# One core, Mamba front end: where the x projection, the high parts, GpSimd's blocks and the statistics stand in the chunk's order

## The reference

```python
x = x + mamba(group_norm(x), ...)        # layer 0
x = x + memory(group_norm(x), m)         # layer 1
```

```python
xn = layer_norm(xf) * ln_w + ln_b                 # 512 channels
xin, z = split(xn @ in_proj_w.T)                  # 1024 channels each
xs = silu(causal_conv4(xin) + conv_b)             # called u in the kernel
x_dbl = xs @ x_proj_w.T                           # 32 columns dt, 16 B, 16 C
delta = softplus(dt @ dt_proj_w.T + dt_proj_b)
# handed on: delta, delta * u, u, silu(z), B, C   -> selective scan, gating, out projection
```

## Time and profile before

| | |
|---|---|
| median of 3 runs | 4889.37 us (4878.66 to 4891.94) |
| the profiled execution's own time | 4877.88 us |
| its span in the trace | 4876.2 us |
| busy: TensorE, VectorE, GpSimd, ScalarE | 95%, 85%, 69%, 61% |
| `front`, from its first projection to the last x_dbl | 73.6 to 1101 us of the span |
| mean granted TensorE clock | 0.984 |

### The profile page before, as it was taken

The page is one execution under the profiler, slowest core; times in us unless marked ns, Lnnn a source line. Parts: engine busy times, 40 slices in busy tenths (PEclk is TensorE's granted clock), DMA queues, the critical chain, the costliest instruction groups (busy, mean ns, idle before and its releaser), DMA issues. The chain is left out here.

```text
span 4876.2 us, 120012 instructions
## 1 busy us (share of the span) xinstructions
PE 4630.9 (95%) x47164; PEld 2943.1 (60%) x47164; DVE 4121.5 (85%) x4361; ACT 2973.5 (61%) x6018; POOL 3367.5 (69%) x1679
## 2 busy tenths in 40 slices
PE   6999899995899999999999999999998899999999
PEld 5666666663455555555555555555554688888787
DVE  7888888878999999999999999999997667677432
ACT  2666666665777767767777777777765445544211
POOL 0667677775999999999999999999997222222000
PEclk9999999997999999999999999999999899999999
DMA  4344444334323332333233323332332111111453
GB/s 168 138 161 161 165 152 152 131 142 158 88 77 97 97 96 80 97 98 97 80 97 97 97 80 97 98 97 80 97 98 78 44 78 78 78 77 78 190 204 140
DMA packets 195579, 538.39 MB, mean 110 GB/s; under 512 B 15904, under 2 KB 15920, under 8 KB 186016
## 3 DMA queue, kind: packets, MB, share of 16 engines
q1 hardware_dynamic: 190144, 482.41, 29.9%
q0 software_dynamic: 4960, 49.25, 2.5%
HBM read 329.22 MB, written 202.38 MB: 109 GB/s over the span
## 5 line engine op out<-in xcount | busy, mean ns | idle before, releaser
L1047 POOL TENSOR_TENSOR sc_hc<-sc_hc,sc_c_rep 128x1024 f32<-128x1024 f32 x1024 | 2396.9, 2368 | 181.8 <-ACT sc_state L1060 179.7
L1248 DVE TENSOR_TENSOR_SCAN sc_hc<-l_m,sc_state,sc_ring 128x512 f32<-128x512 f32 x2048 | 2430.6, 1259 | 24.5 <-PE sc_ring L1171 16.8
L1092 ACT ACTIVATE l_m<-l1s_v,l_neg_a 128x512 f32<-128x512 f32 x2048 | 1351.9, 707 | 0.8 <-DMA l1s_v<-spill 0.8
L1171 PEld LDWEIGHTS sc_ring<-sc_diag,l1s_iota 64*64 64x64 f32 x32768 | 890.5, 133 | 699.4 <-issue 699.4
L1171 PE MATMUL sc_ring<-sc_diag,l1s_iota 64*64 64x128 f32 x32768 | 1104.0, 276 | 9.0 <-DVE sc_hc L1248 6.7
L1181 PE MATMUL sc_y_ps<-sc_hc,sc_fold 128*64 128x512 f32 x4096 | 994.0, 606 | 29.2 <-POOL sc_hc L1047 21.6
L1060 ACT ACTIVATE sc_state<-sc_hc 128x2 f32<-128x2 f32 x1024 | 206.1, 201 | 636.8 <-DVE sc_hc L1248 636.8
L923 PE MATMUL sc_o_ps<-l_et,l_sums 128*128 128x512 f32 x1024 | 559.1, 633 | 11.9 <-ACT l_count L913 11.9
L1508 POOL TENSOR_TENSOR l_count<-l_count,as_oh 128x1024 f32<-128x1024 f32 x64 | 182.4, 2850 | 508.1 <-DVE as_oh L1702 508.1
L1181 PEld LDWEIGHTS sc_y_ps<-sc_hc,sc_fold 128*64 128x64 f32 x4096 | 249.2, 136 | 412.5 <-issue 379.0
L71 PE MATMUL fr_mm<-fr_xn_hi,l0f_w_in_hi 128*128 128x512 f32 x1024 | 432.3, 422 | 27.3 <-DVE fr_delta L708 11.8
(11 more groups left out here) (191 smaller groups left out, 6385.8 us busy)
## 6 DMA issues: line engine op xcount, KB each, us to landing
sc_duz<-spill SPq DMA_DIRECT2D x128, 768.0 KB, 5.9
l1s_v<-spill SPq DMA_DIRECT2D x256, 256.0 KB, 4.0
spill<-fr_z SPq DMA_DIRECT2D x64, 512.0 KB, 2.8
spill<-fr_u SPq DMA_DIRECT2D x32, 1024.0 KB, 9.9
spill<-fr_du SPq DMA_DIRECT2D x32, 1024.0 KB, 4.3
spill<-fr_delta SPq DMA_DIRECT2D x32, 1024.0 KB, 6.5
sc_c_rep<-bc SPq DMA_DIRECT2D x128, 256.0 KB, 4.3
soft<-l_et SPq DMA_DIRECT2D x16, 2048.0 KB, 6.2
```

The lines of the kernel that those rows point to most:

```text
L1047: nc.gpsimd.tensor_tensor(hc[:, p], hc[:, p], c_rep[:, 2 * q:2 * q + 2, :], ALU.mult).then_inc(s_hp, 1)
L1092: nc.scalar.activation(da[:, p % 4, r, :], delta[:, i % 2, p % 2, :], ACT.Exp, scale=keep.neg_a[:, c:c + 1]).then_inc(s_da, 1)
L1171: done = nc.tensor.matmul(to[:, :, k::4], dut[rows, i % 2, k, HALF * h:HALF * h + HALF], diag[rows, u, 4 * q + c:4 * q + 4:2, k, :], start ...
L1248: nc.vector.tensor_tensor_scan(hc[:, p, r, :], da[:, p % 4, r, :], ring[:, SLOT[at], r::2], state[:, i, 2 * p + r:2 * p + r + 1], ALU.mult ...
```

## The change

1. **TensorE's order.** x0, then px7 of g-1, z0, d0..3 of g-1, x1, z1, x2, z2, mean of g+1, d4..7 of g-1, x3, z3, x4, z4, var, x5, z5, px0 px1, x6, z6, px2 px3, x7, z7, px4 px5, px6. So seven of the eight px matmuls move into their own chunk, and px7 stands behind the next x0. `mean` moves one block later, behind z2. z0 moves ahead of d0 to d3, in the ring too.
2. **High parts on ScalarE.** `high` does the four copies, each after the matching slice of z7 was read (new semaphore `s_read`), between keep x7 and `silu_u` of block 6. VectorE keeps the four subtractions.
3. **ScalarE's order.** keep x0, copy_dt, z0, absolutes, exp, log. At the chunk's end: keep x7, the four high parts, u6, z7, u7.
4. **GpSimd in pairs.** The same four operations over two blocks at a time, 128x1024, and semaphores raised by two at the end of the pair.
5. **VectorE's order.** The convolution of block 0 before the four `positive`.
6. **Group parameters in steps.** In the last chunk of entry 0 the group mean's matmul stands after x0, the spread on VectorE after conv 0, the second matmul after d0..3, the root on ScalarE before exp, the scale on VectorE before `rounded`.

```diff
-    ORDER = [("x", 0)] + [("d", m) for m in range(4)] + [("z", 0), ("x", 1), ("z", 1), ("x", 2), ("z", 2)]
+    ORDER = [("x", 0), ("z", 0)] + [("d", m) for m in range(4)] + [("x", 1), ("z", 1), ("x", 2), ("z", 2)]
 # GpSimd
-                for m in range(KD):
-                    n = KD * g + m
+                for m in range(0, KD, 2):
+                    n = KD * g + m + 2
+                    two = slice(m, m + 2)
...
+                    nc.gpsimd.tensor_tensor(du[:, two, :], u[:, two, :], delta[:, two, :], ALU.mult).then_inc(s_du, 2)
 # ScalarE
+            def high(g, before=None):
+                act.wait_ge(s_xn, g + 1)
+                for k in range(KC):
+                    if before is not None and k < KC - 1:
+                        act.wait_ge(s_read, (KC - 1) * before + k + 1)
+                    elif before is not None:
+                        act.wait_ge(s_mm, count(before, "z", KD - 1))
+                    nc.scalar.activation(xn[0][:, k, :], v[:, k, :], ACT.Copy).then_inc(s_xh, 1)
...
+                keep_x(g, 0, ends)
                 if not first:
                     copy_dt(g - 1)
-                keep_x(g, 0, ends)
+                silu_z(g, 0)
...
+                keep_x(g, KD - 1, ends)
+                if after(1):
+                    high(g + 1, g)
+                silu_u(g, KD - 2)
+                silu_z(g, KD - 1)
                 silu_u(g, KD - 1)
 # TensorE
+                project(g, "x", 0, first)
+                if after(1) and after(1)[0] != b:
+                    group_mean(g)
                 if not first:
-                    project_x(g - 1)
-                project(g, "x", 0, first)
+                    project_x(g - 1, KD - 1, KD)
+                project(g, "z", 0, first)
...
                 project(g, "x", 2, first)
+                project(g, "z", 2, first)
                 if after(1):
                     mean(g + 1)
-                project(g, "z", 2, first)
...
+                    if m > 4:
+                        project_x(g, 2 * m - 10, 2 * m - 8)
+                project_x(g, KD - 2, KD - 1)
 # VectorE
+                conv(g, 0)
+                if ends:
+                    group_spread()
                 if not first:
                     for m in range(4):
                         positive(g - 1, m)
-                conv(g, 0)
+                if ends:
+                    group_scale()
```

More of the change, by code:

```diff
@@ L272, in front @@
         s_xn = w.sem("xn_done")
+        s_read = w.sem("xn_read")
         s_xh = w.sem("xn_hi_done")
@@ L283, in front @@
         s_xd = w.sem("xdbl_done")
-        s_one = w.sem("ones_set")
         s_dt = w.sem("dt_copied")
@@ L388, in main @@
                 g = b * NJ + j
-                for m in range(KD):
-                    n = KD * g + m
+                for m in range(0, KD, 2):
+                    n = KD * g + m + 2
+                    two = slice(m, m + 2)
                     pool.wait_ge(s_r, 2 * g + m // 4 + 1)
                     pool.wait_ge(s_ln, 2 * g + m // 4 + 1)
[L393 to L400, removed]
+                    nc.gpsimd.tensor_tensor(du[:, two, :], du[:, two, :], r[:, m % 4:m % 4 + 2, :], ALU.subtract).then_inc(s_c1, 2)
+                    pool.wait_ge(s_c1, n + 4)
+                    nc.gpsimd.tensor_tensor(du[:, two, :], du[:, two, :], e[:, two, :], ALU.add).then_inc(s_c2, 2)
+                    pool.wait_ge(s_rl, n + KD)
+                    pool.wait_ge(s_c2, n + KD)
+                    nc.gpsimd.tensor_tensor(delta[:, two, :], delta[:, two, :], du[:, two, :], ALU.add).then_inc(s_dl, 2)
+                    pool.wait_ge(s_dl, n)
+                    nc.gpsimd.tensor_tensor(du[:, two, :], u[:, two, :], delta[:, two, :], ALU.mult).then_inc(s_du, 2)
             pool.sem_inc(s_c1, 4)
@@ L483, in main @@
                         absolute(g - 1, m)
+                    if after(1) and ends:
+                        group_root()
                     exp(g - 1, 0)
                     log(g - 1, 0)
-                silu_z(g, 0)
                 keep_x(g, 1, ends)
                 silu_z(g, 1)
-                if after(1) and ends:
-                    group_root()
                 keep_x(g, 2, ends)
@@ L504, in main @@
                 silu_u(g, 1)
-                for m in range(3, KD):
+                for m in range(3, KD - 1):
                     keep_x(g, m, ends)
@@ L510, in main @@
                         root(g + 1)
+                keep_x(g, KD - 1, ends)
[3 more added lines that the diff above has]
+                silu_z(g, KD - 1)
                 silu_u(g, KD - 1)
-            act.wait_ge(s_one, 2)
-            act.wait_ge(s_zero, 3)
+            act.wait_ge(s_zero, 5)
             act.sem_inc(s_out, KD)
@@ L521, in _ @@
             root(0)
+            high(0)
             chunks(act, main)
@@ L575, in project @@
                                         [part[:, k, :] for part in xn], k == 0, k == KC - 1)
+                    if (kind, m) == ("z", KD - 1) and k < KC - 1:
+                        last.then_inc(s_read, 1)
                 last.then_inc(s_mm, 5 if first and (kind, m) in (("z", 0), ("z", 2)) else 1)
@@ L583, in project_dt, with project_x @@
                                      dt[row:row + RANK + 1, :], start=True,
[L584 to L588, removed]
+                                     stop=True).then_inc(s_mm, {0: 3, 4: 5}.get(m, 1) if ends else 1)
+            def project_x(g, first, last):
+                if first == 0:
+                    pe.wait_ge(s_dt, g + 1)
+                for m in range(first, last):
                     pe.wait_ge(s_u, KD * g + m + 1 + 2)
-                    last = nc.tensor.matmul(xd_ps[:], keep.w_xp[:, m, :], u[:, m, :], start=(m == 0), stop=(m == KD - 1))
-                last.then_inc(s_xd, 1)
+                    done = nc.tensor.matmul(xd_ps[:], keep.w_xp[:, m, :], u[:, m, :], start=(m == 0), stop=(m == KD - 1))
+                if last == KD:
+                    done.then_inc(s_xd, 1)
             def main(b, j, after, first):
                 g = b * NJ + j
+                project(g, "x", 0, first)
+                if after(1) and after(1)[0] != b:
+                    group_mean(g)
                 if not first:
-                    project_x(g - 1)
-                project(g, "x", 0, first)
+                    project_x(g - 1, KD - 1, KD)
+                project(g, "z", 0, first)
                 if not first:
@@ L600, in main @@
                     project_dt(g - 1, 0, 4)
[L601 to L605, removed]
                 if after(1) and after(1)[0] != b:
                     group_var()
+                project(g, "x", 1, first)
+                project(g, "z", 1, first)
                 project(g, "x", 2, first)
+                project(g, "z", 2, first)
                 if after(1):
                     mean(g + 1)
-                project(g, "z", 2, first)
                 if not first:
@@ L623, in _ @@
             chunks(pe, main)
-            project_x(NG - 1)
+            project_x(NG - 1, KD - 1, KD)
             pe.wait_ge(s_dt, NG + 1)
@@ L635, in _ @@
             for row in (RANK, 64 + RANK):
-                nc.vector.memset(ones[row:row + 1, :], 1.0).then_inc(s_one, 1)
+                nc.vector.memset(ones[row:row + 1, :], 1.0).then_inc(s_zero, 1)
             dve.sem_inc(s_rs, 1)
@@ L676, in normalise, with split @@
                 nc.vector.tensor_tensor(v[:], v[:], over_blocks(rs), ALU.mult).then_inc(s_xn, 1)
[L678 to L683, removed]
+            def split(g):
                 for k in range(KC):
@@ L772, in main @@
                         positive(g - 1, m)
-                conv(g, 0)
+                if ends:
+                    group_scale()
                 if not first:
                     rounded(g - 1, 0)
-                if ends:
-                    group_spread()
-                    group_scale()
                 if after(1):
@@ L806, in main @@
                 if after(1):
-                    split(g + 1, g)
+                    split(g + 1)
             norm_v(0, 0)
```

## The result

The changed kernel takes 4927.15 us (median of 4 runs, 4926.81 to 4932.73) against 4887.01 us: a ratio of 1.0087, 95% interval 1.0069 to 1.0104, or about 40 us slower. The forecast was 4915, slower, within 4862 to 4944. The profiled span grew from 4876.2 to 4925.4 us. All of it is in the front end: the last copy_dt starts at 1153.6 instead of 1101.1 us, and what follows it takes 3771.8 instead of 3775.1 us. The traces show more than the medians: the kernel before was profiled in one of its shorter executions (4877.9 against a median of 4887.0), the kernel after in one at its median, so the two traces lie 49.5 us apart and the medians 40.1.

What follows compares the result with a forecast made beforehand. No engine was full: a loop of waits through ScalarE, GpSimd's chain and TensorE set the 64 us period. Chunks of 67.0, 67.9 and 66.3 us gave +22.4, with +5.2 and -1.6 +26: 4889.4 + 26 = 4915, range 4862 to 4944.

Steps and rivals of the forecast that it cites:

- O: Rival reading in run 1: TensorE's new order alone costs the time, the pairs nothing; within 5 us of 4927.
- P: Rival reading in run 1: GpSimd's longer instructions hold VectorE, which is the bound; same waits before d7, 4897.
- Log to u0: From the first log's end to ScalarE's silu_u of block 0: 11.2 us with the pair, today 7.2.
- X to P: In each chunk, from x0's start to the first log's end: 16.6 us, 3.8 more than today.
- +26: Whole change: +22.4 us from chunk 1 to 15, +5.2 for the last chunk, -1.6 at first chunk and boundary.
- the clock: TensorE's low clock around the wait before d7: 0.85 us lost per chunk, between 0 and 3.
- +12: TensorE's clock: if every chunk lost twice what was taken, the sum would be 12 us higher.
- Pairs on GpSimd: GpSimd's chain: a pair takes 9.74 us instead of 10.86, 4.5 less per chunk; collisions kept at 5.6.
- group parameters in steps: Last chunk of entry 0: scale ready before `rounded`, about 1.6 us left for the root; 67.9 us instead of 73.3.
- A: Rival, faster: the wait at d7 is swallowed and GpSimd's chain stays the bound; 62.7 us period, 4855; chance 0.19.
- C: Rival: the clock falls in full in each chunk; 69 us per chunk, 4945; chance 0.12.
- D: Rival: only the group chunk moves, the rest compensates; -6, 4883; chance 0.24 together with another rival.

Runs made afterwards that it cites:

- run 1: The changed kernel with GpSimd back at single blocks instead of pairs: 4890.54 us, ratio 0.9998 to the kernel before.
- run 2: The changed kernel, pairs kept, with ScalarE's u of block 0 moved behind z2, the second absolutes and the square: 4885.90 us, 0.9996.
- run 6: The changed kernel with GpSimd's blocks 0 and 1 single again and pairs for blocks 2 to 7: 4877.89 us, 0.9980.
- Run 10: The kernel of run 2 with GpSimd's first pair of each chunk placed behind VectorE's four normalisations: 4872.33 us, 0.9964.
- run 5: The kernel before with GpSimd in pairs and nothing else: 4883.53 us, 0.9990.
- run 8: The kernel of run 2 with the order of Run 10, and VectorE's maximum of block 4 alone ahead of the centring: 4877.27 us, 0.9979.
- run 4: The changed kernel with fifteen wide matmuls (128 rows by 512 columns) before d6, filling TensorE's wait before d7: 4918.79 us, 1.0067.
- run 12: The changed kernel with the four high parts back on VectorE, slice by slice behind z7's: 4939.86 us, 1.0110.

## Why the prediction was right, and where it was off

*The mechanism.* The chain du of block 0, u0, z2, d7, x3 is what the trace shows, and runs 1, 2 and 6 each take 36 to 49 us back by cutting it at another place. They leave neither O nor P standing. Log to u0: 11.2 said, 11.6 measured. X to P: 16.6 and 16.8 (397.63 to 414.41, with x0 one period of 68.35 before 465.98). The wait before d7: 5 to 6 said, 5.46 measured, in nine of fifteen chunks; in five it is shared with the mean's, which I had put inside it. No wait at the chunk's end: so.

*The size.* The last copy_dt was to come 26 us later and came 52 later, twice as much. That the median (4927) lies only 12 us above the forecast is in part luck: +26 was worked out on the trace of one of the kernel's shorter executions and added to a median 11.5 us above it. Two terms were mis-sized. The first is the clock: I took 0.85 us per chunk, out of 0 to 3. In the chunk shown x3's start is 0.6 late by the cold d7, and its twelve matmuls take 2.3 more: 2.9. That, with 0.4 for u0 and small gains elsewhere, turns 66.3 into 68.1 in entry 1 and 67.0 into 68.05 in entry 0, together 17 us. In entry 0 the 67.0 was VectorE's stretch, and it did not bind: TensorE's path gives the same 68.05 in both entries. The windows of the earlier trace rows had given 3.3 us for a stretch; the step from there to 0.85, that part of it falls into the waits, was taken without a row. In the kernel before, z2's twelve matmuls behind the 9.18 us wait ran from 544.37 to 549.7, 5.3 us instead of 2.8, which would have given it. What the low clock explains is a part of the way from 64.9 to 68.1, though, and not what sets the changed kernel apart from runs 1, 2 and 6, in which x3 is slow in 13 to 15 chunks as well: there the wait itself was taken away. The Trainium skill's rule on kernels that wait once per tile ("TensorE: Matmul & The Clock Gate", section "HAM oscillation — how this bites in real kernels"), which I weighed at +12, agrees with the trace: x3's twelve matmuls behind the wait take 4.3 to 5.3 us in every chunk.

The second is the collisions under *Pairs on GpSimd*, which I kept at 5.6 us. The chunk of *group parameters in steps* came out as said (68.9; 67.9 said), but chunk 8 gained a 12.14 us wait, 8.9 us over the forecast for it. The collisions are not constant: the four normalisations end in steps of GpSimd's instructions, so that the price grows with GpSimd's instruction (1.92 us alone, up to 4.75 beside single blocks in the kernel before, 10.24 beside pairs). Run 10, which keeps them apart, shows the cause, and run 5 shows the same price in chunk 7 without the new order. The Trainium skill ("GPSIMD Engine Reference", section "8. Key points") names contention of the two engines at shared interfaces, and the 10.24 us agree; how the price grows is from the rows.

*The rivals.* A (GpSimd's chain sets the period, 62.7) was wrong in its premise: 46.2 and not 44.5 from log to chain's end, and TensorE's path is the longer one. Its 4855 does not follow from its terms either: -32, with +5.2 for the last chunk and -1.6, gives 4861. But with u0 moved it is what remains: run 8 waits there. C's period (69) is nearer to the truth than the forecast's own, D's part was real and was given back in chunk 8. The chances have a slip: the forecast's 0.45 and C's 0.12 less 0.03 make 0.54 for slower and not 0.56.

*What stays open.* The exact price of the clock, and why it falls behind waits of 1.1 us in some chunks and not in others. Why chunk 8's tile lands 2 us later than the others, and in runs 4 and 12 does not.

## What to carry to other kernels

Before coarsening an engine's work, ask who waits for its first piece and who for its last: the coarse form delays the first by a whole piece, and may not bring the last sooner. Two changes that each cost nothing can close a loop together, so a prediction needs the order in which instructions stand behind the waiting one. Count the engine's clock behind the waits too, and read it from the rows of single matmuls: here it fell behind short waits as well.

## What the runs showed of the hardware

- VectorE's four normalisations (tensor_scalar, SBUF to SBUF) beside GpSimd's tensor_tensor ran in steps of the GpSimd instruction: 1.92 us for four alone, 10.24 beside 128x1024 ones of 2.4 us. VectorE's convolution steps, whose sum lies in PSUM, kept 2.34 us for three beside the same GpSimd work.
- TensorE busy with matmuls of 33 rows for 12 us had a granted clock of 0.68 on average, after 128-row matmuls at the full clock and with no wait between.
- A wait of 5.46 us was followed by 7 us at 0.50. Waits of 1.1 us, in run 1, were followed by d7 in 1.12 to 2.05 us and by an x3 at 4.2 to 5.3 us in most chunks, at 2.87 in the fifth. In run 4 a wait of 1.65 us behind fifteen matmuls of 128 rows and two of 33 was followed by an x3 at 5.17.
